# Attention in a decoder block: the four products with the values move together into the next group, and the sums are copied out behind the eighth unit

## The reference, cut to what matters

```
q, k = rope(x @ Wqa @ Wqb), rope((x @ Wkva @ Wkvb)[..., 0]);  v = (...)[..., 1]
scores = einsum('bqhd,bkhd->bhqk', q, k) * scale       # 16 heads, 512 x 512, causal
w      = softmax(scores)
out    = einsum('bhqk,bkhd->bqhd', w, v) @ Wout + bout
```

## Time and profile before

| | |
|---|---|
| median of three runs | 1348.08 us |
| profiled execution | 1350.23 us |
| its span (first to last instruction) | 1348.4 us |
| PE busy | 1046.7 us (78%) |
| DVE, ACT, POOL busy | 788.7, 663.5, 425.9 us |
| mean granted PE clock | 0.906 |
| attention, with values: first and last V | 201.8 and 510.7 us |

### The profile page before, as it was taken

The page is one execution under the profiler, slowest core; times in us unless marked ns, Lnnn a source line. Parts: engine busy times, 40 slices in busy tenths (PEclk is TensorE's granted clock), DMA queues, the critical chain, the costliest instruction groups (busy, mean ns, idle before and its releaser), DMA issues. The chain is left out here.

```text
span 1348.4 us, 22433 instructions
## 1 busy us (share of the span) xinstructions
PE 1046.7 (78%) x6749; PEld 751.9 (56%) x6749; DVE 788.7 (58%) x1680; ACT 663.5 (49%) x1166; POOL 425.9 (32%) x556
## 2 busy tenths in 40 slices
PE   3777058788999985783566989899898999988875
PEld 2444023343444433672454877778687786867764
DVE  3888356576777743863444655746656574655523
ACT  1334115565666673461225466473655747465433
POOL 0344226566333331110422231524313242330301
PEclk9677558999999996896777999999999999999987
DMA  2332423333222103257202040301203030020000
GB/s 85 103 116 74 124 92 111 114 120 105 90 96 93 58 31 135 117 223 287 57 26 84 1 125 0 109 16 44 81 0 116 8 108 16 0 78 1 10 7 16
DMA packets 52716, 103.72 MB, mean 77 GB/s; under 512 B 6640, under 2 KB 32496, under 8 KB 48560
## 3 DMA queue, kind: packets, MB, share of 16 engines
q1 hardware_dynamic: 49484, 95.53, 21.0%
q0 software_dynamic: 1920, 6.03, 1.4%
q10 hardware_dynamic: 1252, 1.39, 0.3%
HBM read 62.96 MB, written 39.58 MB: 76 GB/s over the span
## 5 line engine op out<-in xcount | busy, mean ns | idle before, releaser
L804 ACT ACTIVATE p_probs<-p_psS 128x512 f32<-128x512 f32 (+1 forms) x352 | 180.8, 563 | 122.3 <-ACTq L803 120.0
L706 DVE CUSTOM_DVE_ANT_0 p_psA<-p_psA,p_mask 128x512 f32<-128x512 f32 (+1 forms) x256 | 155.5, 647 | 103.9 <-DVEq L704 103.6
L1771 DVE TENSOR_TENSOR p_hl<-p_h,p_hh 128x512 fp32r<-128x512 f32 x128 | 86.9, 688 | 153.1 <-DVEq L1770 151.1
L838 PE MATMUL p_psA<-p_ks,p_qs 96*128 96x512 bf16 (+3 forms) x512 | 144.1, 317 | 37.0 <-PEq L836 36.7
L857 PE MATMUL p_psS<-p_qs,p_ks 99*128 99x256 bf16 (+3 forms) x512 | 131.1, 310 | 20.0 <-PEq L882 11.4
L1656 ACT ACTIVATE p_h<-p_psG,w_columns 128x512 f32<-128x512 f32 x128 | 88.3, 690 | 94.4 <-ACTq L1655 94.0
L725 POOL TENSOR_SCALAR_AFFINE_SELECT p_probs<-p_probs 128x512 f32<-128x512 f32 x128 | 80.8, 635 | 130.8 <-POOLq L724 113.8
L1975 PE MATMUL p_psY<-p_n,p_hh 128*128 128x256 f32 x512 | 105.3, 289 | 12.5 <-PEq L2035 7.6
L868 PE MATMUL p_psO<-p_probs,p_v 128*32 128x512 f32 (+3 forms) x1024 | 92.8, 457 | 26.6 <-PEq L864 25.2
L857 PEld LDWEIGHTS p_psS<-p_qs,p_ks 99*128 99x128 bf16 x512 | 44.0, 98 | 106.8 <-issue 91.8
L1697 ACT ACTIVATE p_hh<-p_h 128x512 fp32r<-128x512 f32 x64 | 40.4, 632 | 118.8 <-ACTq L1696 118.8
(11 more groups left out here) (244 smaller groups left out, 2811.6 us busy)
## 6 DMA issues: line engine op xcount, KB each, us to landing
p_n<-n_parts SPq DMA_DIRECT2D x16, 1024.0 KB, 6.8
o_sums<-p_o SPq DMA_DIRECT2D x32, 256.0 KB, 2.9
n_parts<-p_nh SPq DMA_DIRECT2D x8, 1024.0 KB, 3.9
n_parts<-p_nl SPq DMA_DIRECT2D x8, 1024.0 KB, 6.0
q_parts<-p_part SPq DMA_DIRECT2D x48, 128.0 KB
p_qs<-q_parts SPq DMA_DIRECT2D x32, 192.0 KB
p_x<-in_x_dram SPq DMA_DIRECT2D x8, 512.0 KB, 4.2
p_qs<-q_parts SPq DMA_DIRECT2D x32, 128.0 KB
```

Of the source, the lines that this page charges most:

```text
L706: nc.vector.tensor_tensor_reduce(out=bank[:, 0:w], in0=bank[:, 0:w], in1=mask[:, S - w:S], scale=1.0, scalar=MASKED, op0=ALU.add, op1=ALU.max,
L804: nc.scalar.activation(probs[:, g % 2, at:at + n * w], psS[place(s, turn) % SB][:, 0:n * w], ACT.Exp, scale=SCALE).then_inc(exp_done, 1)
L838: last = nc.tensor.matmul(bank[:, z * w:(z + 1) * w], qs[0:SROWS, k, g * G + r0 + z, i * P:(i + 1) * P], ks[0:SROWS, k, g, 0:w], start=Tru ...
L1771: nc.vector.tensor_tensor(hl[:, s, :], h[:, s, :], hh[:, s, :].bitcast(F32), ALU.subtract).then_inc(h_parts, 1)
```

## The change

Behind S1 of a group PE now does V0 and V1 of the group before, and behind S5 its V2 and V3; no product with the values of a group is left in the group itself. ACT copies the sums out behind its exponential of S7 instead of S4. The wait on the exponentials for V0 is moved with it and asks for nothing that S1 has not asked for. The constant `WAITED` is written in another way and keeps its value, 45. Behind the last group PE does all four products instead of two. The store and the refill on SP stay behind the copy, and are moved with it. Lines of the changed kernel are one higher from the table on (L838 is L839).

```diff
--- before.py
+++ after.py
@@ -587,9 +587,10 @@
         EARLY = 2
         SPLIT_BATCHES = -(-(len(splits) - 2 * EARLY) // (KVH * TT // 2))
 
-        OUT_AT = 4
-        PV2_AT = 2
-        PV0_AT, PV1_AT = 7, 10
+
+
+        PV_AT = {1: (0, 1), 5: (2, 3)}
+        OUT_AT = 7
 
         SUNITS = [(0, r, 1) for r in range(G)] + [(1, r, 1) for r in range(G)] + [(2, 0, 2), (2, 2, 2), (3, 0, 4)]
         LAST = [3, 7, 9, 10]
@@ -871,7 +872,7 @@
                     last.then_inc(O_ready, 1)
 
 
-            WAITED = (KVH - 1) * RING + place(LAST[1]) + 1
+            WAITED = KVH * RING - SB
 
             def batch(k, first, has_next):
                 used = [0 if first else WAITED - KVH * RING]
@@ -901,17 +902,12 @@
                         score_cols(ring(place(s, turn), start), k, g, s)
                         if rows and s in ROWS_AT:
                             score_rows(*ahead, ROWS_AT.index(s))
-                        if s == PV2_AT and (g >= 1 or not first):
-                            for j in (2, 3):
-                                exps(start - RING + place(LAST[j]) + 1)
+                        if s in PV_AT and (g >= 1 or not first):
+                            for j in PV_AT[s]:
+                                if j == 0:
+
+                                    exps(start - RING + place(OUT_AT + 1) + 1)
                                 values(k if g >= 1 else 1 - k, (g - 1) % KVH, j)
-                        if s == PV0_AT:
-
-                            exps(start + place(OUT_AT + 1, turn) + 1)
-                            values(k, g, 0)
-                        if s == PV1_AT:
-                            exps(start + place(LAST[1], turn) + 1)
-                            values(k, g, 1)
                 return KVH * RING - (0 if has_next else 1) - used[0]
 
             for unit in range(len(AUNITS)):
@@ -932,7 +928,7 @@
             left = batch(1, False, False)
             pe.wait_ge(exp_done, left)
             pe.sem_inc(exp_done, -left)
-            for j in (2, 3):
+            for j in range(TT):
                 values(1, KVH - 1, j)
             pe.wait_ge(A_free, 4)
             pe.sem_inc(A_free, -4)
```

## The result

The changed kernel takes 1404.08 us (median of 4 runs, 1401.46 to 1409.34) against 1348.14 (4 runs, 1347.18 to 1355.12): a ratio of 1.0399, interval 1.037 to 1.0428. The forecast was 1377, in a range of 1356 to 1391. The direction was right, and so was the chain that makes the kernel slower; the size was not: +56 us where +29 was forecast.

A forecast was written before the change was run, and what follows sets the result against it. It took PE's chain (18.22 us) and the DMA's (18.43 us) as tied per heavy pair; late refill +20.0, clock +11, rest 0, -2.3 and +0.5 gave +29, so 1377 us, range 1356 to 1391.

The forecast's parts named there:

- The group gets shorter: Steady attention group: moving the value products cuts it from 9.11 to about 8.65 us.
- The waits for masks go: PE before V0 and V1: mask waits like 2.99 us shrink to about 1.4; V0's wait for ACT goes.
- The copy, the store and the refill come later: Eleven pairs with a refill: later store delays the next maxima's DMA behind the refill, 21.15 us a pair, +20.0 us.
- The clock: PE after the new S0 waits: half clock behind two in three, 1.5 us each; +11 us, bounds 0 and +19.
- The rest: Outside the eleven pairs: 0 before 243.68, -2.3 us for four groups after the last refill, +0.5 at the end.
- in time: Rival, 0.11: the maxima land in time and the shorter group is kept; 1332 us.
- partly made up: Rival, 0.10: refill late, but its engines take 10.5 to 11 us instead of 12.45; 1348 to 1356 us.
- The clock falls at each wait, or for twice as long: Rival, 0.08: half clock costs more than the forecast's term, or DVE holds up PE at row units; 1385 to 1400 us.

The follow-up runs named there:

- before_sixteen: The kernel before, with the refill's broadcast loads issued as one DMA per copy; 1313.74 us, ratio 0.9738 to the kernel before.
- warm: The changed kernel with 16 extra, overwritten PE products ahead of the maxima wait at heads of groups 0 and 2, batches 1 to 6; 1376.08 us, ratio 1.0191.
- late_store: The kernel before with only the store of the sums held back to behind ACT's exponential of S9, copy and products unmoved; 1405.74 us, ratio 1.0383.
- maxima_on_act: The changed kernel with the maxima's DMA issued from ACT's queue instead of SP's; 1395.34 us, ratio 1.0334 to the kernel before.
- early_loads: The changed kernel with SP issuing the refill's query and key loads ahead of the store, the values' load staying behind it; 1366.20 us, ratio 1.0117.

## Why the prediction was wrong

By its own steps:

- *The group gets shorter*, to 8.65: the groups behind the last refill, with nothing late, took 8.51, 8.66 and 8.81. Right.
- *The waits for masks go*: 26.6 to 2.4 us ahead of the value products. Right. That they came from POOL's place alone was incomplete: before_sixteen shrinks them without moving a product.
- *The copy, the store and the refill come later*: store at 8.1 behind S0, store to last packet 12.45. At full clock 8.14; from store to last packet 11.8 to 12.4 in the last seven pairs and 13.1 to 14.9 in the first four, 12.8 on average. warm shows this link nearly by itself: 25.4 us over the pairs, or some 24 without the pair that kept its half clock, where 20.0 was forecast. Right in kind and 4 us short; warm's last seven pairs take 21.0 us on average, the first four, in which the DMA share is 0.30 to 0.38 instead of 0.23 to 0.25, 22.7.
- *The clock* is the step that failed: the term had too few waits and too short a slow stretch behind each. The prediction took two waits in three, at 1.5 us each: +11, at most +19. The half clock followed every wait, for 4.6 to 6.4 us of the heavy group in nine of the eleven and 3.3 to 3.4 in two. The heavy stores came 9.45 to 10.96 us behind S0, which is 27 us more in all than eleven times 8.1. warm, without the half clock, has 26 us less in the pairs and 28 in the median. I had sized the term from the earlier trace rows, where the store came 6.75 behind S0 instead of 5.00. The kernel before shows what that 1.75 us paid for, in a window and in ACT's copy of the sums:

```profile
247.50:250.40 2.90, 2.70 (x22) 1.15 (x14) 1.97 (x6) 1.91 (x5) 1.21 (x3) 1.00 0.09 35
...
249.75 0.59 ACT L786 ACTIVATE p_o<-p_psO 128x512 f32<-128x512 f32 x1
```

  The clock was back at 1.00 from 247.50 on, before the copy at 249.75. So 1.75 us was the whole price of a slow stretch of some 3.4 us, and not of a longer one. The two stretches of that length in the changed kernel cost about the same, 9.45 - 8.1 = 1.35 and 9.69 - 8.1 = 1.6 us; the nine longer ones cost 2.2 to 2.9 each. The new place of the copy is the smaller part. late_store has the copy in its old place, in the group whose slow window stands above:

```profile
421.10 0.59 ACT L786 ACTIVATE p_o<-p_psO 128x512 f32<-128x512 f32 x1
```

  That is 421.10 - 414.71 = 6.4 us behind S0 instead of 4.3, so a stretch of about 6 us costs 2.1 us even there, against 2.8 in the changed kernel.
- *The rest*: S0 at 243.68 came at 242.04, -1.6 (forecast 0). From the last heavy pair's end to the last product +4.3 (forecast -1.8): the group at 506.30 has a wait and the half clock as well and takes 10.93 us, where I had counted it as one of four light ones. The phases behind the attention took some 5 us more in this one profiled execution, which is itself 5 us over the median; no run tells what that is.

Together, on the profiled executions: -1.6 + 51.5 + 4.3 + 5 = +59.2, and 1409.34 - 1350.23 = +59.1.

The rivals: *in time* and *partly made up* needed the maxima's packets to end less than 9, or 11, us behind the store; they ended 11.8 to 14.9 behind. *The clock falls at each wait, or for twice as long* is what happened, and both at once; its 1385 to 1400 ends 4 us below the time. With the clock's 27 us in the place of 11 the forecast's own sum is 20 + 27 - 1.8 = +45 us, 1393; most of what is missing is the 4 us of the refill's link and the stretch behind the last heavy pair. The Trainium skill's rule (TensorE: Matmul & The Clock Gate, Part 1: The HAM clock gate), by which each of the waits would cost, agrees with this trace: all eleven did. I had weighed it down by the one wait in three of the earlier trace rows that went free.

Not settled: what decides whether the clock falls behind a short wait, and for how long. It stayed up behind the 2.99 us of the earlier trace rows, 3.07 us in maxima_on_act and 1.82 us in early_loads, and fell behind 1.57 us in early_loads. In the changed kernel it fell for 3.3 to 3.4 us of the group behind waits of 4.54 and 3.85 us, and for 6.1 behind 4.44. The runs give no rule in the wait's length alone.

## What to carry to other kernels

When a step that triggers a DMA moves, follow everything queued behind it to the last packet, and count what else shares its engines: here a store 3.1 us later became a wait of 4.4 us before every second group of PE, though nothing on PE or ACT reads what is stored. When a wait is in a loop and the next trigger stands behind it, let the bound for the clock take every wait as paid, and at the price of the longer slow stretch: here a stretch of 3.4 us cost 1.4 to 1.8 us and one of about 6 us 2.1 to 2.9, and each delay comes back as the next wait. And before tuning around a late DMA, look at its share of the engines: 19.1% is about three of sixteen, and spreading the copies was worth 37 us in the kernel before and 89 in the changed one.

## What the runs showed of the hardware

- In maxima_on_act a small DMA issued on another engine's queue hardly got past the refill: its 48 packets of 256 bytes, issued at 399.22, were moving until after 405.0 between those of the refill, and the kernel gained only 9 us (1404.08 to 1395.34).
- Short waits of PE can cost clock: in early_loads 1.85 us idle, then a granted clock of 0.55 over the next 3.3 us. In warm extra products in the idle time kept it at 1.00 in all pairs but one, and by that work without use the kernel got 2% faster (1404.08 to 1376.08).
- Loads split into one DMA for each copy were done sooner though SP issues twice as many: six of them take 2.7 us to issue instead of 2.2 for three, and the time fell from 1404.08 to 1314.61.
